# An attention block with relative positions: one tile of the distance matrix per group is replaced by six rows of the score product

## The reference, cut to what matters

```python
dist_idx = pos_l - pos_r + M - 1            # M = 256, the table dist_emb has 2 * M - 1 = 511 rows
pos_emb = dist_emb[dist_idx]                # an index past the end reads the last row
rel_q = jnp.einsum('bhld,lrd->bhlr', q, pos_emb)
rel_k = jnp.einsum('bhrd,lrd->bhlr', k, pos_emb)
scores = (scores + rel_q + rel_k) / jnp.sqrt(jnp.asarray(D, scores.dtype))
```

## Time and profile before

| | |
|---|---|
| median of three runs | 2954.4 us |
| the profiled execution's own time | 2954.29 us |
| its span (first to last instruction) | 2952.5 us |
| mean granted TensorE clock | 0.898 of full speed |
| busy: PE, DVE, ACT, POOL | 2521.0, 2049.5, 1623.3, 1896.4 us |
| PE products of the distances, lines 699 and 711 | 8192 |
| bytes read and written in device memory | 417.39 and 352.63 MB |
| stores of the matrix, `r_scratch` | 256 of 1024 KB |
| loads of the matrix, `t_r` | 1024 of 256 KB |

### The profile page before, as it was taken

One profiled execution on the slowest core, in us unless ns is written; L12 is line 12 of the kernel. 1 busy time (PEld: TensorE's weight loads), 2 busy tenths in 40 slices (PEclk: granted clock), 3 DMA queues, 4 the chain that ended last, 5 costly groups with the idle time before them and its releaser, 6 DMA issues. The chain is left out here.

```text
span 2952.5 us, 53450 instructions
## 1 busy us (share of the span) xinstructions
PE 2521.0 (85%) x19084; PEld 1750.5 (59%) x19084; DVE 2049.5 (69%) x5771; ACT 1623.3 (55%) x2069; POOL 1896.4 (64%) x1535
## 2 busy tenths in 40 slices
PE   4877748887887887779999999999999589999998
PEld 2554537776776776646666666666666345555553
DVE  4655526776777677657777777777777478888884
ACT  1443535665655566457878787878788312222222
POOL 2333246466575655478888888888888545566664
PEclk7998957877777777689999999999999799999999
DMA  3577589999999999999999999999999412222210
GB/s 114 185 244 252 172 267 403 395 385 376 390 407 368 400 392 373 386 291 338 309 307 305 303 310 305 301 323 306 307 303 301 143 67 75 82 76 75 75 47 24
DMA packets 301960, 773.59 MB, mean 262 GB/s; under 512 B 37608, under 2 KB 104496, under 8 KB 258048
## 3 DMA queue, kind: packets, MB, share of 16 engines
q1 hardware_dynamic: 276880, 659.84, 65.1%
q10 hardware_dynamic: 18160, 87.26, 9.2%
q0 software_dynamic: 6656, 23.07, 2.2%
HBM read 417.39 MB, written 352.63 MB: 261 GB/s over the span
## 5 line engine op out<-in xcount | busy, mean ns | idle before, releaser
L903 POOL TENSOR_SCALAR t_neg<-t_neg,t_low 128x512 f32<-128x512 f32 x512 | 794.9, 1567 | 120.1 <-DVE t_low L1104 115.8
L1104 DVE CUSTOM_DVE_ANT_1 t_neg<-t_ps,t_r 128x512 f32<-128x512 f32 x1024 | 667.6, 686 | 250.8 <-issue 245.9
L1166 ACT ACTIVATE t_eT<-t_pt 128x1024 f32<-128x1024 f32 x512 | 524.4, 1024 | 212.2 <-PE t_pt L1023 211.5
L1023 PE MATMUL t_pt<-t_ident,t_neg 128*128 128x128 f32 x4096 | 617.3, 273 | 5.2 <-POOL t_neg L903 4.7
L1023 PEld LDWEIGHTS t_pt<-t_ident,t_neg 128*128 128x128 f32 x4096 | 517.0, 142 | 83.1 <-POOL t_neg L903 6.3
L1488 PE MATMUL e_pX<-e_we,e_h2T 128*128 128x512 f32 x1024 | 455.8, 596 | 14.3 <-DVE e_even L1696 14.3
L1011 PE MATMUL t_ps<-t_kb,t_qa 96*128 96x512 bf16 x1024 | 399.2, 390 | 60.7 <-DVE t_low L1104 36.9
L787 DVE TENSOR_TENSOR d_r<-d_pq,d_r 128x1024 f32<-128x1024 f32 x256 | 298.7, 1218 | 149.9 <-ACT d_r L758 123.3
L1156 ACT ACTIVATE t_neg<-t_neg,t_low 128x512 f32<-128x512 f32 x512 | 369.0, 721 | 45.3 <-DVE t_low L1104 45.3
L787 DVE TENSOR_TENSOR ad_nat<-d_pq,ad_nat 128x1024 f32<-128x1024 f32 x256 | 299.3, 1218 | 129.7 <-ACT ad_nat L758 92.1
L659 POOL COPY d_q<-d_q 32x2048 f32<-32x2048 f32 x104 | 196.3, 1888 | 279.3 <-DMA d_q<-q_by_place_scratch 275.8
(11 more groups left out here) (154 smaller groups left out, 3261.5 us busy)
## 6 DMA issues: line engine op xcount, KB each, us to landing
t_r<-r_scratch SPq DMA_DIRECT2D x1024, 256.0 KB, 6.9
r_scratch<-d_r SPq DMA_DIRECT2D x128, 1024.0 KB, 10.1
r_scratch<-ad_nat SPq DMA_DIRECT2D x128, 1024.0 KB, 7.9
d_q<-q_by_place_scratch ACTq DMA_DIRECT2D x52, 256.0 KB, 5.5
ad_nat<-q_by_place_scratch ACTq DMA_DIRECT2D x52, 256.0 KB, 6.3
q_rows_scratch<-a_part SPq DMA_DIRECT2D x16, 768.0 KB, 4.7
k_rows_scratch<-a_part SPq DMA_DIRECT2D x16, 768.0 KB, 3.7
q_by_place_scratch<-ad_nat SPq DMA_DIRECT2D x6, 2048.0 KB, 11.5
```

Of the source, the lines that this page charges most:

```text
L903: nc.gpsimd.tensor_scalar(neg[:, j % RING, t, :], neg[:, j % RING, t, :], low[:, j % RING, t:t + 1], None, ALU.subtract).then_inc(pool_sub, 1)
L1023: last = nc.tensor.transpose(p_t[t // 2][:, t % 2, c, :], neg[:, j % RING, t, c * P:(c + 1) * P], ident[:])
L1104: nc.vector.tensor_tensor_reduce(out=neg[:, j % RING, t, :].rearrange("p (c r) -> p c r", r=TB), in0=p_s[t % 2][:].rearrange("p (c r) -> p ...
L1166: nc.scalar.activation(to, p_t[half][:], ACT.Exp, scale=(1.0 if half else -1.0)).then_inc(exped, 1)
```

## The change

The tiles (0, 3) of both groups, where every distance is past the end, are neither computed nor stored. The snake then has 15 tiles per group; (0, 2) is followed by (1, 3), where q and k both are new. The two vectors are taken from neighbouring tiles: the k part of tile (0, 2) at its last row, l = 383, and the q part of tile (1, 3) at its first column, r = 128, are both at distances that read the table's last row. DVE copies the one from the tile buffer of (0, 2) (one copy, before the adds reach that row) and the other from the 16 q units of tile (1, 3) (one copy each, before the add), splits both into three bf16 parts at the end of tile (1, 3), and SP stores them, beside rows of ones, as `edge_scratch`.

In the attention the rows of q and k grow from 96 to 102: for q the six new rows are (three parts of q.e, one, one, one) at l from 384 on and zero elsewhere, for k (one, one, one, three parts of k.e) at r below 128 and zero elsewhere. They are loaded by ACT, four more loads per batch; the zeros are written once at the stage's start by DVE (q) and POOL (k). The matrix load with rc = 0 leaves out the last 32 partitions, which DVE clears once. The eight semaphores per tile buffer for the stores become one with the same total.

The core of the diff:

```diff
+EDGE = 6
...
 def distances(...)
+        edge = sb("d_edge", [P, 2, TB])
+        edge_rest = sb("d_edge_rest", [P, 2, TB])
+        edge_rows = sb("d_edge_rows", [P, 2, EDGE, TB], BF16)
+        by_row = edge_rows[:].rearrange("n x r l -> n (x r) l")
...
-        r_stored = [[sem(f"d_r_stored{u}_{p}") for p in range(NP)] for u in range(2)]
+        r_stored = [sem(f"d_r_stored{u}") for u in range(2)]
...
+        tiles = [tile for tile in tiles if tile[1:] != (0, NT - 1)]
-        new_k = [i % NT == 0 for i in range(NTILE)]
+        new_k = [i == 0 or tiles[i][:2] != tiles[i - 1][:2] for i in range(NTILE)]
...
 # ACT, before the first copy of a tile
-                        for p in range(NP):
-
-                            later(act, r_stored[i % 2][p], 16 * (i // 2))
+
+                        later(act, r_stored[i % 2], 16 * NP * (i // 2))
...
 # DVE
+                def split_edge(g):
+
+                    NE_STEP = NU + 1 + 3
+                    done = NE_STEP * g + NU + 1
+                    dve.wait_ge(edge_step, done)
+                    later(dve, edge_stored, 16 * g)
+                    nc.vector.tensor_copy(by_row[:, 0::9, :], edge[:]).then_inc(edge_step, 1)
+                    dve.wait_ge(edge_step, done + 1)
+                    nc.vector.tensor_tensor(edge_rest[:], edge[:], by_row[:, 0::9, :], ALU.subtract).then_inc(edge_step, 1)
+                    dve.wait_ge(edge_step, done + 2)
+                    nc.vector.tensor_copy(by_row[:, 1::9, :], edge_rest[:]).then_inc(edge_step, 1)
+                    dve.wait_ge(edge_step, done + 3)
+                    nc.vector.tensor_tensor(by_row[:, 2::9, :], edge_rest[:], by_row[:, 1::9, :], ALU.subtract
+                                            ).then_inc(edge_done, 1)
+
+                nc.vector.memset(edge_rows[:], 1.0)
+                for i, (g, rc, lc) in enumerate(tiles):
                     dve.wait_ge(k_out, NU * (i + 1))
                     for n in range(NU):
+                        part = r[i % 2][:, n * QL:(n + 1) * QL, :]
+                        if (rc, lc) == (0, NT - 2):
+                            if n == 0:
+
+                                later(dve, edge_done, g)
+                                nc.vector.tensor_copy(edge[:, 1, :], r[i % 2][:, TB - 1, :]).then_inc(edge_step, 1)
+                            if n == NU - 1:
+                                dve.wait_ge(edge_step, (NU + 4) * g + 1)
                         dve.wait_ge(q_units, NU * i + n + 1)
+                        if (rc, lc) == (1, NT - 1):
+
+                            nc.vector.tensor_copy(edge[:, 0, n * QL:(n + 1) * QL], pq[n % 2][:, :, 0]).then_inc(edge_step, 1)
                         nc.vector.tensor_tensor(part, pq[n % 2][:], part, ALU.add).then_inc(q_added, 1)
+                    if (rc, lc) == (1, NT - 1):
+                        split_edge(g)
...
 # SP
+                    if (rc, lc) == (1, NT - 2):
+                        sp.wait_ge(edge_done, g + 1)
+                        sp.dma_start(edge_d[g], edge_rows[:]).then_inc(edge_stored, 16)
...
 def attention(...)
-        qa = sb("t_qa", [ROWS, 1, SLOTS, S], BF16)
-        kb = sb("t_kb", [ROWS, 1, SLOTS, S], BF16)
+        qa = sb("t_qa", [ROWS + EDGE, 1, SLOTS, S], BF16)
+        kb = sb("t_kb", [ROWS + EDGE, 1, SLOTS, S], BF16)
-        BATCH = 16 * (len(T_Q_LOADED) + len(T_K_LOADED))
+        BATCH = 16 * (len(T_Q_LOADED) + len(T_K_LOADED) + 2)
+        Q_EDGE, K_EDGE = slice(S - TB, S), slice(0, TB)
+        EP0 = P - TB // TT
...
 # POOL, before the first copies
+                for u in range(2):
+                    nc.gpsimd.memset(kb[ROWS:ROWS + EDGE, 0, u * H:(u + 1) * H, TB:S].bitcast(F32), 0.0).then_inc(k_zeroed, 1)
+                pool.wait_ge(k_zeroed, 2)
...
 # SP, load_r
-                        sp.dma_start(r[:, n % RR, c].rearrange("p t r -> p (t r)"), src).then_inc(r_loaded[n % RR], 16)
+                        rows = EP0 if c == 0 else P
+
+                        sp.dma_start(r[0:rows, n % RR, c].rearrange("p t r -> p (t r)"), src[0:rows]
+                                     ).then_inc(r_loaded[n % RR], 16)
...
 # PE, before the first product
+                pe.wait_ge(q_zeroed, 2)
+                pe.wait_ge(k_zeroed, 2)
...
 # DVE, before the first copies
+                for u in range(2):
+                    nc.vector.memset(qa[ROWS:ROWS + EDGE, 0, u * H:(u + 1) * H, 0:S - TB].bitcast(F32), 0.0).then_inc(q_zeroed, 1)
+                nc.vector.memset(r[EP0:P, :, 0], 0.0).then_inc(r_zeroed, 1)
+                dve.wait_ge(r_zeroed, 1)
...
 # ACT
+                def load_edge(b, half, x):
+                    tensor, columns = ((qa, Q_EDGE), (kb, K_EDGE))[x]
+                    first = H // 2 * half
+                    n = b % GB * H + first
+                    at = b % 2 * H + first
+                    act.dma_start(tensor[ROWS:ROWS + EDGE, 0, at:at + H // 2, columns],
+                                  edge_d[b // GB, n:n + H // 2, x].rearrange("n r l -> r n l")).then_inc(batch_loaded[half], 16)
...
                                 load(b + 1, at // len(pieces), at % len(pieces))
+                                if at % len(pieces) < 2:
+                                    load_edge(b + 1, at // len(pieces), at % len(pieces))
...
+                    for x in range(2):
+                        load_edge(0, half, x)
```

More of the change, by code:

```diff
@@ L589, in _, with distances @@
                 empty_parts(nb - 1, 1)
-def distances(nc, tab_d, n_d, r_d, nat, stored, ng=NG):
+def distances(nc, tab_d, n_d, r_d, edge_d, nat, stored, ng=NG):
     n_stored = stored[0]
@@ L781, in _ @@
             def _(dve):
-                for i in range(NTILE):
+                def split_edge(g):
[13 more added lines that the diff above has]
+                for i, (g, rc, lc) in enumerate(tiles):
                     dve.wait_ge(k_out, NU * (i + 1))
                     for n in range(NU):
+                        part = r[i % 2][:, n * QL:(n + 1) * QL, :]
[5 more added lines that the diff above has]
+                                dve.wait_ge(edge_step, (NU + 4) * g + 1)
                         dve.wait_ge(q_units, NU * i + n + 1)
-                        part = r[i % 2][:, n * QL:(n + 1) * QL, :]
+                        if (rc, lc) == (1, NT - 1):
+                            nc.vector.tensor_copy(edge[:, 0, n * QL:(n + 1) * QL], pq[n % 2][:, :, 0]).then_inc(edge_step, 1)
                         nc.vector.tensor_tensor(part, pq[n % 2][:], part, ALU.add).then_inc(q_added, 1)
+                    if (rc, lc) == (1, NT - 1):
+                        split_edge(g)
             @block.sync
@@ L799, in _, with attention @@
                                      r[i % 2][:, p * PART:(p + 1) * PART, :].rearrange("n l r -> n (l r)")
-                                     ).then_inc(r_stored[i % 2][p], 16)
+                                     ).then_inc(r_stored[i % 2], 16)
                 for u in range(2):
-                    for p in range(NP):
-                        sp.wait_ge(r_stored[u][p], 16 * NTILE // 2)
-def attention(nc, rows_d, v_d, r_d, cT_d, nb=NB):
+                    sp.wait_ge(r_stored[u], 16 * NP * NTILE // 2)
+                sp.wait_ge(edge_stored, 16 * NG)
+def attention(nc, rows_d, v_d, r_d, edge_d, cT_d, nb=NB):
     ctx = ExitStack()
@@ L854, in attention @@
         batch_loaded = [sem(f"t_batch_loaded{i}") for i in range(2)]
-        BATCH = 16 * (len(T_Q_LOADED) + len(T_K_LOADED))
+        BATCH = 16 * (len(T_Q_LOADED) + len(T_K_LOADED) + 2)
+        Q_EDGE, K_EDGE = slice(S - TB, S), slice(0, TB)
+        EP0 = P - TB // TT
+        q_zeroed = sem("t_q_zeroed")
+        k_zeroed = sem("t_k_zeroed")
+        r_zeroed = sem("t_r_zeroed")
         K_PLACES, Q_FIRST = (10, 12, 15, 18), 10
@@ L1737, in program @@
     r_d = [scratch(f"r{g}_scratch", [NT, P, RPITCH]) for g in range(NG)]
+    edge_d = scratch("edge_scratch", [NG, P, 2, EDGE, TB], BF16)
     modulation(nc, ins, mod_d, tab_d)
@@ L1750, in program @@
         projections(nc, ins, mod_d, h_d, n_d, rows_d, v_d, nat, stored)
-        distances(nc, tab_d, n_d, r_d, nat, stored)
-    attention(nc, rows_d, v_d, r_d, cT_d)
+        distances(nc, tab_d, n_d, r_d, edge_d, nat, stored)
+    attention(nc, rows_d, v_d, r_d, edge_d, cT_d)
     experts(nc, ins, mod_d, h_d, cT_d, out)
```

3 lines of the change are left out of this document (added).

## The result

The changed kernel takes **3038.6 us**, the median of four runs (3025.1 to 3051.9), against 2953.1 (2950.7 to 2954.8) for the kernel before: a ratio of 1.029, 95% interval 1.0238 to 1.0342. The forecast was 2914, the range 2902 to 2932. Not only the size is wrong but the sign, and the cause is none of the rivals.

A forecast was written before the change was run, and what follows sets the result against it. The prediction took DVE's add chain and the DMA queue to bound the distances, and PE to be nearly full in the attention. -48.4 + 5.4 + 1.9 + 1.0 = -40.1 from 2954.3 gave 2914 us, range 2902 to 2932.

The forecast's parts named there:

- Item 1: Distances: dropping tile (0,3) of both groups saves 24.2 us per group, ends 20.4 and 29.7; -48.4 us in all.
- Item 2: Distances, tile (1,3): 16 small DVE copies of 192 ns per group, plus a row copy of 0.2 us; +5.4 us.
- Item 3: End of tile (1,3): the split into three parts takes under 1.7 us, covered by DVE's 4.9 us idle; nothing added.
- Items 4 and 5: Distances: storing the edge vectors adds 1.9 us; one shared semaphore per buffer in place of eight adds nothing.
- more gained: Rival, distances: small copies hide and the second group's late tile goes whole; 2902 us, chance 0.10.
- Item 6: Attention's opening: clearings stay hidden, but the first half waits for 8 loads instead of 6; +1.0 us, ends -1 and +4.
- Item 7: Attention, steady: smaller r loads, 64 more ACT issues (end +20 us) and 102-row score products (end +1) all change nothing.
- cost nothing visible: Attention: four heads take 16.26 us while ACT issues the next batch's loads, 16.41 without, so loads issued there are free.
- Item 7, the rest: Attention, steady: 64 more ACT issues cost nothing (end +20 us); 102-row products and their weight loads cost nothing (end +1).
- The slower one: Rival, attention: the score's weight load stops hiding under the transpose, +116 us, 3030 us; chance 0.07, including costlier ACT issues.
- Queue or POOL limits: Rival, distances rows 0 and 1: only the bytes' 20.4 us per group go, or less; 2922 to 2928 us, chance 0.22.
- nothing saved: Rival, distances: the dropped tile's time returns as store waits of tile (1,3); 2954 us plus 0 to 5, chance 0.03.

The follow-up runs named there:

- experiment 1: Kernel before with only the row block 0 matrix load cut to 96 of 128 partitions, the rest cleared once: 3065.6 us against 2952.0.
- experiment 3: Changed kernel with row block 0 matrix loads on all 128 partitions, the last 32 read as zeros stored during the projections: 2934.1 us, ratio 0.9935 against the kernel before.
- experiments 1, 2 and 4 to 11: Row block 0 matrix load altered in partitions, bytes or row order, against the kernel before; 2: changed kernel, edge loads only for batches 0 and 1. 2948.2 to 3138.6 us.
- experiment 7: Kernel before with the row block 0 matrix load cut into two loads of 64 alternate partitions, even and odd: 2955.0 us against 2955.2.

## Why the prediction was wrong, point by point

- **Item 1, the tile: right.** -48.4 forecast. 480 adds, 272 copies on POOL, tiles mostly still 23.2 to 24.7 us apart where no k is loaded.
- **Item 2, the small copies: right.** 160 ns where 192 was taken; tile (1,3) takes 26.6 us where it took 24.5, and 27.0 in the second group where it took 24.0, the 2 to 3 us named. The row copy took 1.7 and 1.0 us where 0.2 was taken: the row of 422 ns was a bad guide.
- **Item 3, the split: right in effect, wrong in size.** Its operations take 0.7 to 1.2 us each, some 4.3 us together, where 1.7 was the most. They still fit under the 4.9 us that DVE waited there.
- **Items 4 and 5** don't show apart. The first five items together: -41.1 forecast, -47.3 measured, between the forecast and *more gained*. Since items 2 and 3 cost no less than was forecast, item 1 gave more than its 24.2 a group, inside its end of 29.7.
- **Item 6, the opening:** +1.0 forecast, +3.9 measured, its upper end of +4. The clearings stayed hidden.
- **Item 7 is the step that failed**, in the sentence "r loads carry 16.8 MB less; nobody waits for them there, so nothing". That nobody waited was true, and the price was taken from it: zero, with no upper end. What the runs showed in its place: with one load of 96 partitions per head, all that the DMA engines move together falls from 307 to about 260 GB/s, +113.6 us alone (experiment 1), and undoing it gives 104 us back (experiment 3). It was also not seen how little room there was. The share was 1.00 at 299 GB/s. The changed kernel's 1.197 MB per head at 4.07 us a head need 294 GB/s, and 257 came: the stage is bound by its loads. The ring of six heads that hid them covers a late load, not a lower rate.
- **What the earlier trace rows hid.** The kernel before has compact loads too: those of q and k, on 32 and 16 partitions, one per head in heads 0 to 11. Over its batches 2 to 13 all that the DMA engines move is 291 to 299 GB/s in those heads and 340 in heads 12 to 15, where there are none, at a DMA share of 0.99 to 1.06. The adds kept 16.3 us per four heads, so "cost nothing visible" was right of the time and not of the rate. That the compact q and k loads are the reason is not tested. In experiment 1 the same stretches move 277, 247, 245 and 275 GB/s, and the four heads from 12 on let SP make up ground; that fits the first four heads of a batch at 16.3 us.
- **Item 7, the rest:** the product and its weight load cost next to nothing, right. The edge loads cost some 22 us of the steady part (experiments 1 and 3), where nothing was taken, although the end named for their issues was +20. The row that carried it, shows loads of q and k with 32 and 16 rows, not of six, and it shows the pace of the adds, not the rate of the loads.
- **The rivals.** The slower one put the loss in the right stage and on the wrong engine: weight load 113 ns, unchanged. *Queue or POOL limits*, *more gained* and *nothing saved* all speak of the distances, and none was asked of the loads that shrink in the attention.

The 96-partition load stood in the change's description, and the Trainium skill has a page that bears on it. "SBUF — State Buffer", section "Door 1: The DMA port swizzle (why [64,N] ≈ [32,N])", says that a partition's number decides by which of 16 ports a transfer reaches it and that partitions 0 to 63 reach only half of them. The rule of the Trainium skill, in that page's section "Summary: rules for kernel authors", is to use 128 partitions in one DMA. The runs agree on the half: the lower one costs 58.6 us, and the even partitions, which by that map reach all 16 ports, cost nothing. But by the same map partitions 0 to 95 and 0 to 111 reach all 16 ports too, and here they cost 113.6 and 129.2 us. How many ports a load reaches does not explain the load that failed.

In the same page of the Trainium skill, "Can I just issue two DMAs to hit both halves?" says no, and the two halves at +186.5 us agree with that. It also says that only one transfer spanning all 128 partitions reaches all ports at once. Here the measurement goes beyond it: two loads of alternate partitions cost nothing (2955.0 against 2955.2).

The Trainium skill, "DMA: Bandwidth & Descriptors", section "The descriptor swizzle", offers a possible reason: in a load of 128 partitions each of the 16 DMA engines writes the partitions of one port, the first eight engines in the lower half and the others in the upper. If the rows of a smaller load are dealt out to the engines in order, a compact part hands some engines partitions of the other half, and alternate partitions leave every engine in its own. The longer packets fit that two engines then meet at one port. This is argued, not shown: no view names the DMA engine of a packet.

**What stays open:** why the rate is the same 257 to 264 GB/s for every compact part, and why the small edge loads cost what they do. A spread load of 96 partitions in four issues a head wasn't tried, and the runs of experiments 1, 2 and 4 to 11 are single ones; their large differences (58 us and more) are far above the spread, the small ones are not.

## What to carry to other kernels

Count the partitions of every load that a change trims. A load that covers only a compact range can slow all loads beside it; reading zeros on all 128 partitions meant 16.8 MB more stored and 16.8 MB more loaded, and was 104 us faster. "Nobody waits for it" holds for one load at the rate of before, so ask also what becomes of the stage at a lower rate: bytes per step over GB/s, beside the time of a step. And take the DMA share with the GB/s, never alone.

## What the runs showed of the hardware that was not expected

- The DMA share doesn't tell a good rate from a bad one: 1.02 at 307 GB/s and 1.05 at 260.
- 64 partitions in one load: the even ones leave 256 KB loads beside them landing after 4.6 us, the lower half after 8.3.
- Packets slow down one by one: 2 KB took 129 ns instead of 106 with a compact load among them, at nearly the same DMA share.
- The issuing queue has a limit of its own: with six loads of the matrix a head SP issued them at a median of 0.58 to 0.59 us, waited 29.5 of 1000 us and held the stage at 256 GB/s and a share of 0.87; with five (experiment 7) it kept up.
- Two loads of 24 KB on six partitions per batch, issued in heads 12 and 13 of 16, made the next batch's first product late each time: 67.0 us in 14 waits, 4.8 us each.
